# A graph network on one core: GpSimd gathers eight attention tiles during the preparation, and ScalarE takes over half of a histogram's digits

## The reference

```python
q = (x @ qW + qb); k = (x @ kW + kb); v = (x @ vW + vb)        # 8 heads of 16
scores = sum(q[src] * k[dst]) / sqrt(D) + edge_attr @ eW + eb   # one per edge and head
attn = softmax over the edges of one dst
out = segment_sum(v[src] * attn, dst) @ oW + ob
x = layernorm(x + L0(x)); then L1 (mean of neighbours), L2 (gated, 3 rounds), L3 (mean)
counts = segment_sum(1, dst)                                     # the histogram
```

## Time and profile before

| | us |
|---|---|
| median of 3 runs | 5863.32 (5856.84 to 5889.07) |
| span of the profiled execution, first to last instruction | 5467.9 |
| first column counted to last column counted | 16.3 to about 91 |
| last store of `prepare` issued | 106.41 |
| first and last ACT q of the attention phase | 135.15 and 679.07 |

### The profile page before, as it was taken

The page is one execution under the profiler, slowest core; times in us unless marked ns, Lnnn a source line. Parts: engine busy times, 40 slices in busy tenths (PEclk is TensorE's granted clock), DMA queues, the critical chain, the costliest instruction groups (busy, mean ns, idle before and its releaser), DMA issues. The chain is left out here.

```text
span 5467.9 us, 75482 instructions
## 1 busy us (share of the span) xinstructions
PE 4078.4 (75%) x16190; PEld 2396.2 (44%) x16190; DVE 3926.0 (72%) x13570; ACT 2937.1 (54%) x6438; POOL 3513.2 (64%) x3137
## 2 busy tenths in 40 slices
PE   5777749999996556547775779977997669946763
PEld 3343425555553333325553445544444334426662
DVE  7677749999997444438896786557765888847762
ACT  0667637788784010128885445534443555537763
POOL 4777758888885888847776760037303775876566
PEclk8888869999998777779998999999998999979996
DMA  6233333333332334348886785458644666758841
GB/s 230 80 88 89 82 73 107 113 112 110 115 110 77 63 61 63 61 75 244 245 246 187 205 218 149 133 168 243 186 143 146 192 185 181 211 165 273 254 130 58
DMA packets 785243, 802.40 MB, mean 147 GB/s; under 512 B 138080, under 2 KB 551848, under 8 KB 784666
## 3 DMA queue, kind: packets, MB, share of 16 engines
q1 hardware_dynamic: 403802, 393.43, 24.7%
q0 software_dynamic: 117504, 209.42, 16.1%
q10 hardware_dynamic: 263488, 194.72, 10.8%
HBM read 445.32 MB, written 351.92 MB: 146 GB/s over the span
## 5 line engine op out<-in xcount | busy, mean ns | idle before, releaser
L476 PE MATMUL gate_bank<-gate_ht,gate_whh 128*128 128x512 f32 x1764 | 872.8, 611 | 45.6 <-DVE gate_n L546 45.6
L476 PEld LDWEIGHTS gate_bank<-gate_ht,gate_whh 128*128 128x128 f32 x1764 | 326.4, 196 | 438.2 <-issue 322.7
L944 POOL DMA_INDIRECT xh<-mean_xh,mean_pos_all x392 | 378.0, 964 | 209.5 <-issue 125.1
L2081 PE MATMUL back_ps_sums<-back_same,back_rows 128*128 128x512 f32 x400 | 287.4, 885 | 287.8 <-DMA back_rows<-x_a,back_idx 287.8
L1464 POOL DMA_INDIRECT ffn_rows<-att_sums,ffn_idx x392 | 394.5, 1006 | 124.1 <-issue 108.2
L291 POOL DMA_INDIRECT gate_rows<-h_a,by_pos x200 | 199.4, 997 | 392.3 <-POOLq L118 326.5
L472 PE MATMUL gate_bank<-by_rank,gate_win 128*128 128x512 f32 x882 | 436.1, 594 | 0.8 <-DVE by_rank L355 0.8
L612 ACT ACTIVATE gate_n<-gate_n,gate_b_ih 128x512 f32<-128x512 f32 x294 | 212.6, 723 | 367.5 <-issue 200.9
L1516 PE MATMUL ffn_ps_f<-ffn_hg,ffn_f 128*128 128x512 f32 x784 | 387.1, 596 | 1.4 <-ACT ffn_hg L1699 1.4
L1509 PE MATMUL ffn_ps_u<-ffn_xs_t,ffn_up_w 128*128 128x512 f32 x784 | 386.8, 595 | 1.1 <-ACT ffn_xs_t L1727 1.1
L2062 POOL DMA_INDIRECT back<-back_out,back_dest x200 | 324.4, 1622 | 67.8 <-issue 60.1
(11 more groups left out here) (272 smaller groups left out, 11740.1 us busy)
## 6 DMA issues: line engine op xcount, KB each, us to landing
mean_x<-x_a SPq DMA_DIRECT2D x196, 256.0 KB
back<-blank ACTq DMA_DIRECT2D x99, 264.0 KB, 4.8
mean_rows<-back SPq DMA_DIRECT2D x98, 264.0 KB
hp<-mean_xh SPq DMA_DIRECT2D x98, 264.0 KB, 4.5
gate_x<-xh SPq DMA_DIRECT2D x98, 264.0 KB, 3.2
gate_hot<-hot_rows SPq DMA_DIRECT2D x100, 256.0 KB, 4.0
ffn_x<-in_x_in SPq DMA_DIRECT2D x98, 256.0 KB
ffn_xr<-in_x_in SPq DMA_DIRECT2D x98, 256.0 KB
```

The source lines that it names most:

```text
L476: last = nc.tensor.matmul(bank_[:, :], whh[:, c * D:(c + 1) * D], ht[:, t.slot4, :], start=not inputs, stop=True)
L944: nc.gpsimd.indirect_dma_start(out=g["xh"][:, :], out_offset=bass.IndirectOffsetOnAxis(ap=pos_all[:, t.n, j:j + 1], axis=0), in_=xh[:, t.n ...
L2081: last = nc.tensor.matmul(ps_sums[t.slot][:, :], rows[:, t.slot4, j, :], same[:, t.slot, j, :], start=j == 0, stop=j == J - 1)
```

## The change

A new class, `AttentionFeed`, owns the attention phase's gather buffers, row numbers and weights. It is made before `prepare`, so that both phases can use it. The ring has 12 tiles in place of 4. In `prepare`, SP first loads all row numbers at once (they are laid out anew on the host: [P, ET*J*2]), and later the eleven weights. POOL gathers tiles 0 to 7 in `prepare`, and no longer makes digits. In `attention_pass` POOL gathers tiles 8 to 49, waiting for `rows_turned` of tile n-12. In the histogram DVE makes the high rows of columns 0 and 3 of each four, and ACT those of columns 1 and 2, with the square of (digit - value) and then relu(1 - square). ACT's part of the program stands behind its 99 stores.

```diff
+    SLOTS, AHEAD, LOADS = 12, 8, 11
+    def gather(self, n):
+        slot = n % self.SLOTS
+        for j in range(J):
+            for col, rows, sem in ((1, self.send, self.sent), (0, self.recv, self.received)):
+                self.nc.gpsimd.indirect_dma_start(
+                    out=rows[:, slot, j, :], out_offset=None, in_=self.g["x_in"][:, :],
+                    in_offset=bass.IndirectOffsetOnAxis(ap=self.idx[:, n, j, col:col + 1], axis=0)
+                ).then_inc(sem[slot], 16)
...
 attention_pass, gpsimd
-                    wait(pool, idx_loaded[t.slot4], 16 * (t.u4 + 1))
-                    wait(pool, rows_turned, t.n - 1)
+            for n in range(feed.AHEAD, ET):
+                wait(pool, rows_turned, n + 1 - slots)
+                feed.gather(n)
...
 Histogram
+    def high_hots_act(self, act, group, digits, one):
+        scalar = self.nc.scalar
+        first, pair = 4 * group + 1, self.apart[:, group % 2, :, :]
+        wait(act, self.high_done_act, group - 1)
+        for k in range(2):
+            last = scalar.activation(pair[:, k, :], digits[:, 0:2 * self.rows], ACT.Square,
+                                     bias=self.high_less[:, first + k:first + k + 1])
+        last.then_inc(self.apart_done, 1)
+        wait(act, self.counted, first + 2 - self.HOT_BUFFERS)
+        act.wait_ge(self.apart_done, group + 1)
+        b = first % self.HOT_BUFFERS
+        scalar.activation(self.hot_high[:, b:b + 2, :].rearrange("p b n -> p (b n)"),
+                          pair.rearrange("p b n -> p (b n)"), ACT.Relu,
+                          bias=one[:, 0:1], scale=-1.0).then_inc(self.high_done_act, 1)
 prepare, sync
+            feed.load_lists(sp)
...
+            feed.load_weights(sp)
 prepare, scalar: behind the stores
             for t in range(NT + 1):
                 act.dma_start(g["back"][t * SUPER:(t + 1) * SUPER, :].rearrange("(p j) d -> p (j d)", j=J),
                               g["blank"][:, :]).then_inc(g["back_blank"], 16)
+            act.wait_ge(ones_set, 1)
+            act.wait_ge(digits_done, 1)
+            act.wait_ge(nodes.split_done, 3)
+            for group in range(ECOLS // 4):
+                nodes.high_hots_act(act, group, digits, ones)
 prepare, gpsimd
-            for c in range(0, ECOLS, 4):
-                nodes.high_hot(pool, nc.gpsimd, c, digits, nodes.high_done_pool)
+            pool.wait_ge(feed.idx_loaded, 16)
+            for n in range(feed.AHEAD):
+                feed.gather(n)
 prepare, vector
-                if c % 4:
+                if c % 4 in (0, 3):
```

More of the change, by code:

```diff
@@ L1088, in _, with __init__, sb, sem @@
             over_tiles(act, NT, 6, step)
-def attention_pass(nc, name, g):
+class AttentionFeed:
+    SLOTS, AHEAD, LOADS = 12, 8, 11
+    def __init__(self, nc, ctx, g):
+        self.nc, self.g = nc, g
+        def sb(name, shape, dt=F32):
+            return ctx.enter_context(nc.sbuf_tensor(f"feed_{name}", shape, dt))
+        def sem(name):
+            return nc.alloc_semaphore(f"feed_{name}")
+        self.idx = sb("idx", [P, ET, J, 2], I32)
+        self.send, self.recv = (sb(n, [P, self.SLOTS, J, D]) for n in ("send", "recv"))
+        self.qw, self.kw, self.vw, self.ow = (sb(n, [P, D]) for n in ("qw", "kw", "vw", "ow"))
+        self.qb, self.kb, self.vb = (sb(n, [P, 1]) for n in ("qb", "kb", "vb"))
+        self.ew, self.eb_row = sb("ew", [EDIM, HEADS]), sb("eb_row", [1, HEADS])
+        self.ob, self.blocks = sb("ob", [P, D]), sb("blocks", [P, HEADS, HEAD_DIM])
+        self.idx_loaded, self.w_loaded = sem("idx_loaded"), sem("w_loaded")
+        self.sent, self.received = ([sem(f"{n}{b}") for b in range(self.SLOTS)] for n in ("sent", "received"))
+        self.semaphores = [self.idx_loaded, self.w_loaded] + self.sent + self.received
+    def load_lists(self, sp):
+        sp.dma_start(self.idx[:, :, :, :].rearrange("p s j c -> p (s j c)"), self.g["edge_blocks"]
+                     ).then_inc(self.idx_loaded, 16)
+    def load_weights(self, sp):
+        g = self.g
+        for dst_, src_ in ((self.qw[:, :], g["qW"]), (self.kw[:, :], g["kW"]), (self.vw[:, :], g["vW"]),
+                           (self.ow[:, :], g["oW"]), (self.qb[:, :], column(g["qb"])),
+                           (self.kb[:, :], column(g["kb"])), (self.vb[:, :], column(g["vb"])),
+                           (self.ew[:, :], g["eW"]), (self.ob[:, :], on_all(g["ob"])),
+                           (self.eb_row[:, :], g["eb"].rearrange("(a n) -> a n", a=1)),
+                           (self.blocks[:, :, :], g["blocks_c"])):
+            sp.dma_start(dst_, src_, allow_slow_non_contiguous=True).then_inc(self.w_loaded, 16)
+    def gather(self, n):
[6 more added lines that the diff above has]
+                ).then_inc(sem[slot], 16)
@@ L1762, in __init__ @@
             f.sem(f"{name}_{s}") for s in ("split_done", "high_done", "low_done", "counted"))
-        self.high_done_pool = f.sem(f"{name}_high_done_pool")
+        self.high_done_act, self.apart_done = (f.sem(f"{name}_{s}") for s in ("high_done_act", "apart_done"))
+        self.high_less = f.sb(f"{name}_high_less", [P, ECOLS])
+        self.apart = f.sb(f"{name}_apart", [P, 2, 2, 2 * rows], BF16)
         (self.count, self.cum, self.has, self.last_e, self.moved, self.picked, self.clipped) = (
@@ L1823, in make_pointers, with prepare @@
                              ALU.add).then_inc(self.lists_made, 1)
-def prepare(nc, name, g):
+def prepare(nc, name, g, feed):
     rows, width = ECOLS // 2, 2 * P
@@ L2197, in build @@
         g["back_blank"] = nc.alloc_semaphore("back_blank")
-        prepare(nc, "prepare", g)
-        attention_pass(nc, "attend", g)
+        with ExitStack() as early:
+            feed = AttentionFeed(nc, early, g)
+            prepare(nc, "prepare", g, feed)
+            attention_pass(nc, "attend", g, feed)
         ffn_pass(nc, "ffn", g)
```

68 lines of the change are left out of this document (23 added, 45 removed).

## The result

| | before | changed |
|---|---|---|
| median, lowest and highest of 4 runs, us | 5871.55 (5856.84 to 5889.07) | 5946.9 (5937.53 to 5949.69) |
| time over that of before | 1 | 1.0131, 95% interval 1.0111 to 1.0151 |

The change costs 1.3%; 5873 and no change were predicted. The profiled execution of the changed kernel took 5949.58 us with a span of 5947.8, so only 1.8 us lie outside the span. That speaks against one reading ahead of the prediction, that the 395.4 us between the span of before and its median lie around the program. The kernel before was profiled again among the experiments: a span of 5857.1 in a time of 5858.99 us.

What follows compares the result with a forecast made beforehand. It took DVE to bound the histogram and ACT's loop, right behind POOL's gathers, the attention phase. +69.4 - 18.5 - 8.5 - 33 = +9.4 us took the span from 5467.9 to 5477; with 395.4 around it, 5873 us, range 5832 to 5908.

Steps and rivals of the forecast that it cites:

- 1 to 3, histogram: Preparation: ACT's late start, ACT's pace and PE's low clock together lose 69.4 us (ends 43 and 89).
- 4, seam: Between preparation and attention phase: weights and tiles already there bring the first q 18.5 us earlier (17 to 19).
- 5, fill: First four attention steps: 40.8 us shortened by 8.5 (6 to 9), as waits for gathered rows go.
- 6, 45 steps: Other attention steps: ACT's loop sets 10.45 us a step instead of 11.18, a gain of 33 us.
- Step 1: Preparation: ACT's digits wait behind 99 stores, slowed by gathers and loads; 74.7 + 14.5 = 89.2 us (76 to 95).
- Steps 2 and 3: Histogram: ACT takes 1.37 us a group, 68.5 for fifty; PE's low clock at restart adds 1.5 us.
- The other sum in step 2: Histogram: by the Trainium skill's activation costs, a group takes 1.31 us plus the wait, 3 us less in all.
- The base: Whole program: the 395.4 us between profiled span 5467.9 and the median stays, added to 5477 for 5873 us.
- PE's clock: Attention phase: granted clock averages 0.83 at 300 to 400 us; rivals: stays up, 5830 us (0.16), stays low, 5907 (0.22).
- the stores did hold ACT: Preparation: the rival that stores don't hold ACT had it free at 37 us, 5821 us in all; chance 0.04.
- DVE and GpSimd hardly block one another: Histogram: the rival had gathers and DVE rows holding each other up, gathers 1.0 us longer, still 5873; no chance given.
- The rival "slower": Attention phase: PE's clock stays low, steps stay at 11.2 us, sum +43, 5907 us; chance 0.22 (slower overall 0.27).

Runs made afterwards that it cites:

- e3: Changed kernel with no tile gathered in the preparation, all 50 in the attention phase, same ring of 12; ratio 1.0239 to the kernel before.
- e4: Changed kernel with POOL held two tiles ahead in the attention phase (rows_turned of tile n-2, not n-12); ratio 1.0067 to the kernel before.
- e5: Changed kernel with all high digits by DVE and two early tiles, gathered behind the last histogram column; ring of 12 free; ratio 1.0124 to the kernel before.
- e6: As e5, with POOL also held two tiles ahead in the attention phase; ratio 0.9971 to the kernel before.
- e10: As e5, with each gather waiting for the landing of the gather two before it; ratio 1.0036 to the kernel before.
- e1: Changed kernel with all high digits made by DVE, early gathers kept; ratio 1.0099 to the kernel before.
- e8: As e1, with four early tiles and a waited-for memset behind each early gather, no wait for landing; ratio 1.0133 to the kernel before.
- e7: As e1, with three early tiles, each early gather waited for until it landed; ratio 1.0112 to the kernel before.

## Why the prediction was wrong

Up to the first ACT row of the next phase the changed kernel is 894.32 - 817.33 = 77.0 us later than before; the medians differ by 75.4. So all of it lies in the first two phases. By the prediction's steps:

| step | predicted | measured | off by |
|---|---|---|---|
| 1 to 3, histogram (pos 106.40 to 190.34) | +69.4 | +83.9 | +14.5 |
| 4, seam (28.5 to 9.5 us from pos to q0) | -18.5 | -19.0 | -0.5 |
| 5, fill (q0 to q4, 51.1 to 87.2) | -8.5 | +36.1 | +44.6 |
| 6, 45 steps (549.2 to 525.6) | -33 | -23.5 | +9.5 |
| behind it (82.1 to 81.6) | 0 | -0.5 | -0.5 |
| sum | +9.4 | +77.0 | +67.6 |

*Step 1, "ACT is free at 89.2".* The mechanism, ACT behind its stores, was right; the term of 14.5 us for the gathers' and loads' bytes measured 27.7. Spaced gathers would cost about what I put, 11 to 15 us for 64; tightly issued ones cost 26 to 29. Steps 2 and 3 were right: 1.41 us a group for 1.37, and e3 ends 1.7 us from the sum. (The other sum in step 2, "3 us less in all", leaves out its own wait of 0.05 us a group; with it, it is 0.5 us less.)

*Step 5, "the first four steps take 32.3".* This is the step that failed: they took 87.2. I looked for waits that go away, for rows, and those did go. The hand-over from PE to ACT and DVE I had put at nothing. A ring of 12 lets POOL gather without waiting, and in this state PE's signals reach ACT and DVE up to 32 us late. e4 shows it by one wait put back (q0 to q4 in 28.6 us, 3.7 less than I predicted), e5 against e6 shows it without early gathers beside the histogram, and e10 with the ring's freedom kept. The same cause stretches the histogram wherever it doesn't wait for ACT (e1); in the changed kernel ACT's slowness hid that.

*Step 6, "10.45 us a step".* 525.6/45 = 11.7, which is 55 us too long in all; the table shows only 9.5 because the steps of the kernel before, too, were 46 us longer than in the rows that I read. So the small error of this row is luck. PE waits for no gathered row between 200 and 700 us, as predicted. Once POOL's last gather is out at 687.4 the steps take 10.0 and 10.5 us in turn, what I had put for all of them; while it gathers, odd steps of 20 us remain (20.2, 20.7), as in the kernel before (18.7, 19.5).

*The base.* I took 395 us of difference between a span and a median for time around the program. The timed executions were longer by about that much, and the rows that I read had none of the late signals, which the second profile has in nearly all phases. That they make up all of the 389 us is not shown. Every term that I took as "before minus after" came from an execution without the trouble. What makes one execution free of it stays open; it is also the one with nearly twice the records of semaphores.

*The rivals.* None had this. The seam, -19.0 for -18.5, was right for the reason given. PE's clock, 0.84 in 300 to 400 us, is what it was in the earlier trace rows; the stores did hold ACT; DVE and GpSimd hardly block one another over gathers, though they do over memsets (e8). The rival "slower" came nearest by its number, 5907, by a wrong way: its steps of 11.2 us.

What is shown, for executions that have the trouble: the delay depends on POOL's gathers and on how tightly they follow one another; it is the signal that is late and not PE's work (e1 at 93.6 us); it strikes above all what waits for PE, and at the onset also what PE waits for; it needs no busy DMA engines; and with about two gathers open it is the spacing that decides (e8, and e1 from 60 us). What is not shown is why close gathers hold the signals. The rival that nobody tested is the recording. The timed executions of the changed kernel and of the experiments are listed with a span and a granted clock, so they too were recorded in some way, and every execution whose late signals could be seen was recorded by the profiler, with about half the semaphore changes of the clean one, and in the histogram of e1 (16 to 91 us) only 113 against 2149 in e7. A program timed without any recording might not lose this time. Three or more gathers open, each waiting for an earlier one, weren't tried.

## What to carry to other kernels

A queue that is given more buffers stops waiting, and its waits may have been what left room for others: before giving GpSimd a deeper ring of gathers, try the deeper ring with the old wait. If engines that wait for PE idle behind matmuls that have ended, while GpSimd issues gathers 0.3 us apart, space the gathers (a wait for the landing of an earlier one) or put them where PE signals seldom. First make sure that the loss is there without a profiler as well, which was not done here. And a median that stands far over the span of the profiled execution can mean a different execution and not time around the program: profile again before subtracting.

## What the runs showed of the hardware

In profiled executions, PE's completions reached DVE or ACT one each 5 to 5.6 us while GpSimd issued 128-row gathers each 1.25 us, those behind queueing up to 43 us (e1); the onset came some 19 us after the first gather (e1, at 22.8). In the first 20 us of it DVE's signals reached PE up to 9.4 us late; after that ACT to PE and DVE to PE took 0.05 to 0.3 us in the same stretches. One execution of the kernel before shows none of this with 400 such gathers in a row. ACT's 99 stores, in another queue, were slowed too, from 72 to 98 to 101 us of issuing, with the DMA engines at 0.66 to 0.73 of their time. A gather with a memset of 1024 elements behind it on GpSimd made two of DVE's `tensor_scalar` rows take 1.7 to 1.8 us instead of 0.28; a gather alone made one take 0.42 to 0.46 (e7).
